# Token stage: the next image's row norm placed between the adds of this image's last products, GELU results in two buffers, tokens taken two images ahead

## The reference

```python
t = x.reshape(B, H * W, dim)                       # after the group norm
t = gelu(t @ W1 + b1); t = gelu(t)                 # 48 -> 16, GELU twice
x1, x2 = t[..., :8], t[..., 8:]
n = layernorm(x2, gamma, beta)                     # over 8 numbers: the "row norm"
sp = depthwise_conv3x3(n) + dw_b                   # the "band"
ch = conv1x1(n) + pw_b
out = (x1 * (sp * ch)) @ W2 + b2                   # 8 -> 48, added to x
```

## Time and profile before

| | us |
|---|---|
| median of 3 runs (2686.31 to 2691.76) | 2691.73 |
| the profiled execution, its own time | 2685.25 |
| its span in the trace | 2683.4 |
| TensorE busy | 2388.4 (89%) |
| VectorE busy | 1330.0 (50%) |
| ScalarE busy | 798.8 (30%) |
| GpSimd busy | 211.3 (8%) |

### The profile page before, as it was taken

How to read it: one execution, slowest core, us unless ns; L and a number is a source line. 1 busy time by engine, 2 the same in 40 slices (tenths; PEclk the granted TensorE clock), 3 DMA queues, 4 the chain that set the end, 5 groups by cost and what they waited for, 6 DMA issues and landing times.

```text
span 2683.4 us, 45712 instructions
## 1 busy us (share of the span) xinstructions
PE 2388.4 (89%) x18588; PEld 2129.1 (79%) x18588; DVE 1330.0 (50%) x3212; ACT 798.8 (30%) x1240; POOL 211.3 (8%) x260
## 2 busy tenths in 40 slices
PE   1999999999999999999999991799999999943785
PEld 1999957956963499999999991799999999942453
DVE  3323344345346544444555558544444555567855
ACT  3533354344245530244002443300441000002441
POOL 2000000000000181000000006300000000000321
PEclk9999999999999999999999996899999999976898
DMA  8840000004000440000000007500000000049734
GB/s 151 154 86 8 1 1 1 1 1 90 6 1 0 94 72 1 1 1 1 1 1 1 1 1 239 126 1 1 1 1 1 1 1 1 1 129 278 240 110 125
DMA packets 80040, 129.89 MB, mean 48 GB/s; under 512 B 10577, under 2 KB 59953, under 8 KB 76945
## 3 DMA queue, kind: packets, MB, share of 16 engines
q1 hardware_dynamic: 72544, 123.36, 19.2%
q10 hardware_dynamic: 7184, 3.84, 0.6%
q0 software_dynamic: 128, 0.01, 0.0%
HBM read 76.85 MB, written 50.33 MB: 47 GB/s over the span
## 4 chain that ended last, share of the span: by engine, by line
PE 82%; DVE 9%; ACT 3%; DMA 2%; SPq 1%; issue 1%; POOL 0%; ACTq 0%; DVEq 0%; POOLq 0%
PE bank L1003 18%; PE bank L1004 16%; PE bank L1005 16%; PE bank L904 14%; PE bank L966 6%; PE bank L919 3%; PE bank L909 3%; DVE stats L1133 3%; ACT work L665 3%; PE bank L1111 2%; DMA work<-in_x 1%; SPq L355 1%; PE bank L1082 1%; DVE band L1252 1%; DVE image L1342 1%
## 5 line engine op out<-in xcount | busy, mean ns | idle before, releaser
L1328 DVE TENSOR_TENSOR image<-bank,image 112x128 f32<-112x128 f32 x2032 | 660.5, 325 | 712.6 <-PE bank L1005 712.6
L1003 PE MATMUL bank<-image,scan_wt 112*112 112x128 f32 x4064 | 810.5, 280 | 9.8 <-ACT image L762 6.7
L1004 PE MATMUL bank<-image,scan_wt 112*112 112x126 f32 x4064 | 771.7, 271 | 0.0
L1005 PE MATMUL bank<-image,scan_wt 112*112 112x126 f32 x4064 | 770.7, 270 | 0.0
L1004 PEld LDWEIGHTS bank<-image,scan_wt 112*112 112x112 f32 x4064 | 581.9, 176 | 0.0
L1005 PEld LDWEIGHTS bank<-image,scan_wt 112*112 112x112 f32 x4064 | 579.4, 176 | 0.0
L1003 PEld LDWEIGHTS bank<-image,scan_wt 112*112 112x112 f32 x4064 | 567.2, 175 | 15.3 <-ACT image L762 7.1
L665 ACT ACTIVATE work<-image,gn_shift,gn_scale 48x567 f32<-48x567 f32 (+5 forms) x384 | 334.9, 905 | 329.4 <-PE bank L909 220.4
L904 PE MATMUL bank<-work 112*128 112x192 f32 x2304 | 422.9, 332 | 10.5 <-issue 10.5
L904 PEld LDWEIGHTS bank<-work 112*128 112x128 f32 x2304 | 374.0, 192 | 12.9 <-issue 12.5
L758 ACT COPY work<-image 48x256 f32 x192 | 80.4, 419 | 686.0 <-PE bank L1005 685.6
(11 more groups left out here) (154 smaller groups left out, 1498.8 us busy)
## 6 DMA issues: line engine op xcount, KB each, us to landing
work<-saved SPq DMA_DIRECT2D x64, 384.0 KB, 9.3
image<-flat_rows SPq DMA_DIRECT2D x4, 3072.0 KB, 18.5
out<-image SPq DMA_DIRECT2D x8, 1536.0 KB, 7.3
flat_rows<-image SPq DMA_DIRECT2D x46, 192.0 KB, 6.5
saved<-image SPq DMA_DIRECT2D x20, 384.0 KB, 8.1
band<-in_x SPq DMA_DIRECT2D x16, 384.0 KB, 5.6
work<-in_x SPq DMA_DIRECT2D x16, 384.0 KB, 5.8
saved<-image SPq DMA_DIRECT2D x8, 768.0 KB, 8.1
```

Source lines behind the costliest of these rows:

```text
L1003: mm(dst, wt[:, 1], src, start=True, stop=False)
L1004: mm(dst[:, 1:J2, :], wt[:, 0], src[:, 0:J2 - 1, :], start=False, stop=False)
L1005: mm(dst[:, 0:J2 - 1, :], wt[:, 2], src[:, 1:J2, :], start=False, stop=True).then_inc(s_prod[g], 1)
L1328: v.tensor_tensor(line(g, along_w, at), prod, line(g, along_w, src), ALU.add).then_inc(s_state[g], 1)
```

## The change

The hidden values get two buffers: `hid[0]` in the free columns behind image 0's tokens, as before, and `hid[1]` in those behind image 2's. All sixteen token groups of image 1 run before the loop over images, with its GELU behind them. The groups of image 2 stand in image 0's second half of products, two behind each product. Those of image 3 stand eight ahead of image 1's gate turn and eight in image 1's first half of products, two behind each of the last four. Each image's hidden values are turned one image earlier. The four parts of the next image's row norm stand behind certain adds, by the table `AHEAD` (key: half f and product q; value: part); for image 3 the first two parts stand ahead of image 2's gate. ScalarE's queue is rearranged to match.

```diff
-EARLY = 12
+AHEAD = ({(0, 0): (0,), (0, 2): (1,), (0, 6): (2,), (1, 1): (3,)},
+         {(0, 0): (0,), (0, 2): (1,), (0, 6): (2,), (1, 1): (3,)},
+         {(0, 0): (2,), (0, 3): (3,)},
+         {})
...
-        hid = image[:, TCOLS:IMG]
+        hid = [image[:, i * 2 * IMG + TCOLS:(i * 2 + 1) * IMG] for i in range(2)]
...
-            def mlp(b, more, even_more):
-
+            def take_hidden(b):
+                if b == 1:
+                    act.wait_ge(s_flat[1][0], 32 * (NBLK - 1))
+                    act.wait_ge(s_taken, 4)
                 for i in range(2):
                     act.wait_ge(s_hid_t, b * 4 + (i + 1))
-                    nc.scalar.copy(*hidden_views(i)).then_inc(s_hid_a, 1)
-                for g in range(6 if more else 0):
-                    take_tokens(b + 1, g)
+                    nc.scalar.copy(*hidden_views(b, i)).then_inc(s_hid_a, 1)
+
+            def row_deviation(b):
                 act.wait_ge(s_ln, b * 2 + 1)
                 nc.scalar.activation(s4, s3, ACT.Sqrt).then_inc(s_ln_a, 1)
-                for g in range(6, EARLY if more else 0):
-                    take_tokens(b + 1, g)
+
+            def mlp(b):
 
                 act.wait_ge(s_ln, b * 2 + 2)
                 nc.scalar.copy(n_pad[:, :, 1:1 + W].rearrange("p c (q w) -> p q c w", q=NQ),
                                spm.rearrange("p (q c w) -> p q c w", q=NQ, c=G)).then_inc(s_ln_a, 1)
                 take_turned(b, 1, n_t)
-                for g in range(EARLY, GROUPS if more else 0):
-                    take_tokens(b + 1, g)
+                if b == 1:
+                    gelu_twice(2)
+                    affine(3)
+                    take_hidden(2)
+                    for g in range(8):
+                        take_tokens(3, g)
+                if b == 2:
+                    take_hidden(3)
+                    row_deviation(3)
                 take_turned(b, 7, g_t)
                 if b == 0:
                     deviation(7, 2, NB, 128)
-                if more:
-                    gelu_twice(b + 1)
-                if even_more:
-                    affine(b + 2)
+                    take_hidden(1)
+                    affine(2)
+                    row_deviation(1)
+                    for g in range(GROUPS):
+                        take_tokens(2, g)
+                if b == 1:
+                    for g in range(8, GROUPS):
+                        take_tokens(3, g)
+                    row_deviation(2)
+                    gelu_twice(3)
...
+            take_hidden(0)
+            for g in range(6):
+                take_tokens(1, g)
+            row_deviation(0)
+            for g in range(6, GROUPS):
+                take_tokens(1, g)
+            gelu_twice(1)
             for b in range(NB):
-                mlp(b, b + 1 < NB, b + 2 < NB)
+                mlp(b)
...
+            def tokens(b, g0, g1, flush=True):
 
                 for g in range(g0, g1):
-                    turn_tokens(g)
-                    if g % 4 == 0 and g > g0:
-                        hidden(g // 4 - 1)
-                hidden(g1 // 4 - 1)
-
-            def mlp(b, more):
-
-
+                    turn_tokens(b, g)
+                    if g % 4 == 0 and g and g != 8 * (b == 3):
+                        hidden(b, g // 4 - 1)
+                if flush:
+                    hidden(b, g1 // 4 - 1)
...
+            def turn_hidden(b):
                 pe.wait_ge(s_gelu, b * 5 + 5)
                 for i in range(4):
                     for t in range(4):
                         o = i * 512 + t * 128
                         last = nc.tensor.transpose(bank[2 + i][:, t * 128:(t + 1) * 128], hid_t[:, o:o + 128], ident)
                     last.then_inc(s_hid_t, 1)
-                if more:
-                    pe.wait_ge(s_xn, b + 2)
-                    tokens(b + 1, 0, EARLY)
+
+            def mlp(b):
...
                     if q % 4 == 3:
                         last.then_inc(s_gt_p, 1)
+                if b == 2:
+                    turn_hidden(3)
                 pe.wait_ge(s_add, b * 2 * NQ + TWO)
                 pe.wait_ge(s_ln_a, b * 2 + 2)
...
-                if more:
+                if b < 2:
+                    turn_hidden(b + 1)
+                if b == 1:
                     pe.wait_ge(s_pw_used, b * 2 + 2)
-                    tokens(b + 1, EARLY, GROUPS)
+                    pe.wait_ge(s_xn, 4)
+                    tokens(3, 0, 8)
 
                 pe.wait_ge(s_gate, b + 1)
...
+                        if b == 0 and f == 1:
+                            if q == 0:
+                                pe.wait_ge(s_xn, 3)
+                            tokens(2, 2 * q, 2 * q + 2, q == NQ - 1)
+                        if b == 1 and f == 0 and q >= 4:
+                            o = 8 + 2 * (q - 4)
+                            tokens(3, o, o + 2, q == NQ - 1)
 
             pe.wait_ge(s_xn, 1)
-            tokens(0, 0, GROUPS, False)
+            tokens(0, 0, GROUPS)
             pe.wait_ge(s_band, N_BAND + G + 1)
-            mlp(0, True)
-            for b in range(1, NB):
-                mlp(b, b + 1 < NB)
+            turn_hidden(0)
+            pe.wait_ge(s_xn, 2)
+            tokens(1, 0, GROUPS)
+            for b in range(NB):
+                mlp(b)
...
-            def mlp(b, more, behind=None):
-
-                for i in range(4):
-                    row_norm(b, i)
-                    if behind and i < 2:
-                        behind(NBLK + 3 + i)
-                for t in range(5, NBLK if behind else 0):
-                    last = behind(NBLK + t)
-                    if t == NBLK - 1:
-                        last.then_inc(s_taken, 2)
+            def mlp(b):
+
+                if b == 2:
+                    row_norm(3, 0)
+                    row_norm(3, 1)
...
                                         ALU.add).then_inc(s_add, 1)
+                        for i in AHEAD[b].get((f, q), ()):
+                            row_norm(b + 1, i)
...
-            mlp(0, True, rows_stats)
-            for b in range(1, NB):
-                mlp(b, b + 1 < NB)
+            for i in range(4):
+                row_norm(0, i)
+                if i < 2:
+                    rows_stats(NBLK + 3 + i)
+            for t in range(5, NBLK):
+                last = rows_stats(NBLK + t)
+            last.then_inc(s_taken, 2)
+            for b in range(NB):
+                mlp(b)
```

## The result

| | kernel before | changed kernel |
|---|---|---|
| median of 19 runs, us | 2689.18 (2683.94 to 2695.04) | 2700.73 (2694.99 to 2709.59) |
| ratio, 95% interval | 1 | 1.0044 [1.0035, 1.0053] |
| profiled execution: span, its own time, us | 2683.4, 2685.25 | 2702.6, 2704.45 |
| token stage: first norm copy to the end, us | 204.51 | 215.60 |

The account below looks back on a forecast made before the run. In the token stage neither TensorE nor VectorE is full: row norm, turn, band, gate and products with adds run one behind the other. Six terms sum to +6.7 us on 2688.8, giving 2696; range 2687 to 2706.

Parts of the forecast that it names:

- start: First norm copy to image 0's first product: GELU ahead of the padding copy delays band and gate; +6.0, bounds +5.0 and +7.1.
- image 0: First product to the next turn: TensorE bounds the second half; 36.5 us against 34.40, +2.1, bounds 33.2 and 39.0 us.
- image 1's turn: Turn to first product: eight groups of image 3 delay the gate's turn; +6.8, bounds +6.3 and +7.5, called the surest.
- image 2: Its turn to image 3's turn: 38.6 us against 45.59, -7.0, bounds 36.4 and 41.5; includes 1.3 more beside GpSimd.
- much slower: Rival: TensorE falls towards half clock in every product stage; +15 in the middle, +19.6 at most, 2704 us; chance 0.18.
- image 1's products: First product to the next turn: square root queued behind the last token copy; 33.0 us against 32.37, +0.6.
- Image 3: Its turn to the end: turn and band no longer follow a 15 us stop; -1.8, bounds -1.8 and 0.
- Without a term: Second hidden buffer and earlier residual loads on SP's queue: no lasting wait added, loads stay hidden, so no time counted.
- The table load: Table switches on ScalarE: 1.28 us each without drain; the skill's drain rule would add 4.1, making the sum near +11.
- Faster: Rival: VectorE sets the pace in both product stages, token groups riding in TensorE's waits; -13.8, 2675 us; chance 0.10.
- No change: Rival: TensorE stays at 2.4 GHz and GpSimd misses the norm; -0.1, 2689 us; chance 0.18.
- the change doesn't do what it says: Rival: second hidden region comes free late, GELU results wait and all slides back; 2689 us; chance 0.04.

Follow-up runs that it names:

- kernel 1: Changed kernel with image 1's two GELUs moved on ScalarE's queue behind image 0's padding copy and n copies: 2696.26 us, 1.0019 to the kernel before.
- kernel 5: Changed kernel with the edits of kernel 1, kernel 2, kernel 3 and kernel 4 together: 2679.80 us, 0.9962 to the kernel before.
- kernel 8: kernel 5 with GpSimd's b2 additions for images 1 to 3 also held until that image's row norm is done: 2679.60 us, 0.9954 to the kernel before.
- kernel 7: Changed kernel with 32 unread transposes filling TensorE's wait for image 0's padding copy, ahead of the band: 2699.04 us, 1.0031 to the kernel before.
- kernel 4: Changed kernel with image 2's token groups behind image 0's products five to twelve, and image 1's square root after two copies: 2694.97 us, 1.0018 to before.
- kernel 2: Changed kernel with no image 3 token groups ahead of image 1's gate turn, all sixteen behind its products five to twelve: 2697.87 us, 1.0031 to before.
- kernel 3: Changed kernel with image 2's square root moved ahead of the last six token copies on ScalarE: 2697.57 us, 1.0032 to the kernel before.
- kernel 6: Changed kernel with GpSimd's b2 additions for images 1 to 3 held until that image's row norm is done: 2695.70 us, 1.0014 to before.

## Why the prediction was right and wrong

The sign and the places were right: the time lies in the range, and three of the six terms came out within 1 us. The size was 11.1 in place of 6.7. The missing 4.4 is start +2.8, image 0 -2.2, image 1 +0.6 (0.8 and -0.2) and image 2 +3.1, each rounded. Three stretches came out above the bounds that I gave them: the start (+8.8 against at most +7.1), image 1's turn (+7.6 against +7.5, the term that I called the surest) and image 2 (41.73 against 41.5). In time the result lies nearer to the middle of the rival "much slower" (2704) than to the forecast (2696); what speaks against that rival is two stretches, image 0 and image 1's products, for which it had +4.6 and +4.5 at the most, and which came out at -0.1 and +0.4.

*Start: mechanism right, +6.0 against +8.8.* The step that failed is "the last token copy ends near 2496.6", 17.7 behind the first norm copy. The trace has 2506.9, or 19.9. What the step left out is TensorE's clock in the groups: where they ran at full speed, in kernel 1, the copy ended at 17.73. In the changed kernel the last eight groups come right behind a wait of 3.40 for a token copy that stood behind the square root (2496.05), and begin at a granted clock of 0.52, near the 1.2 GHz level: four transposes take 1.09 where they take 0.64 elsewhere. Then GELU takes 5.2 as worked out, and the padding copy starts 25.13 behind the norm copy instead of 16.72. The band waits 4.22, as forecast, and takes 7.19 at 0.57; I had put up to 1.8 for that, and taken less. So 8.4 comes through the queue and the slow groups, 1.7 from the band (7.19 less 5.52), and the gate gives back some 1.1 without GpSimd beside it, as forecast (its last step takes 1.88 in place of 3.04). Kernels 1, 5 and 8 show the order as the cause, and kernel 7 prices the clock in the band at 2.3 to 2.9.

*Image 0: +2.1 against -0.1, the low part of its bounds.* Its second half is bound by TensorE as forecast: from 2547.4 to 2567.4 it is busy 17.27 of 20.00 us, and in kernel 4, where part of this work moves forward, the stretch is 3.3 shorter. The tenth product goes 17.15 behind the first (2550.26), between the 16.1 and 19.9 of the working, and the rest takes 17.15 on 18.2 of counted work. The 2.2 that I had put on top of this for GpSimd and the clock is what was too much. GpSimd's addition (2540.46 to 2554.8) fell on parts 2 and 3 instead of part 1, where they lie mostly beside the groups, and these ran at 2.4 GHz (1.00 over the same 20 us) in place of the slow beginning that I had allowed for.

*Image 1, turn to first product: mechanism right, +6.8 against +7.6.* The affine ends 12.5 behind the turn (2579.91), as worked out from rows of before; the gate's turn starts at 21.8 instead of the 20.9 of the sum, since the first groups behind the wait of 2.65 ran slowly (granted 0.93 over the stretch). In kernel 1, at 1.00, the stretch takes 21.90. Kernel 2 takes the groups away and gives 7.2 back.

*Image 1, products: right, +0.6 against +0.4.* The root behind the last copy cost 5.25 of waiting, and kernel 3 gives back 4.3. The lower bound was 30.6 with this wait and no slow clock; the other 2.1 fits with TensorE's 0.50 in 2597 to 2602, where four multiplies take 2.93 instead of 1.57 (12.60 / 8), and with the last step of part 0, which takes 2.17 instead of 1.23 beside GpSimd's addition (2584.29 to 2595.75). No run separates these two.

*Image 2: the mis-sized term, -7.0 against -3.9.* The step was "beside GpSimd 1.3 more". L1466, L1468 and L1469 take 2.47, 2.46 and 3.02 beside the addition, and 1.23, 1.22 and 1.87 without it: 3.6. I had scaled from one operation of the earlier trace rows, where three were in the way. The trace of before had the price: L1429 takes 2.49 there, and its like L1431 1.23 in the earlier trace rows; each of the three should have carried the difference. The Trainium skill, "SBUF — State Buffer", "SBUF: two separate sides", states the rule that I didn't weigh: VectorE operations with two SBUF inputs and GpSimd share a pair of ports under a lock that one instruction holds to its end, and the other blocks. This case agrees: the two-column operation ahead of the stage ends with GpSimd's addition both times (1658.85 and 1658.83, 1660.40 and 1660.38), and here each of the three pays 1.15 to 1.24, less than one of GpSimd's eight instructions alone (11.46 / 8 = 1.43), while RECIPROCAL (one input; 0.95) and the adds (one input in PSUM, the banks that TensorE writes; 0.56) pay nothing. The remaining part of the term was right in kind: products behind waits of 3 and 4 us start slowly, and when the waits shrink the stretch falls to 35.60 (kernel 6), under my lower bound of 36.4.

*Image 3: right, -1.8 against -1.77.* The turn takes 1.04 in place of 1.97 and the band 5.56 in place of 6.46, as worked out.

*Without a term: right.* Image 1's norm copies (2535.36) start as its first add ends, so the hidden results weren't late, and image 3's addition on GpSimd ends at 2657.5, ahead of its first add at 2682.6.

*The table load.* The Trainium skill, "ScalarE: Activation LUTs", "What ACT_TABLE_LOAD costs", would have made the sum +11, which is what was measured. That is chance: GELU again began 1.30 behind the start of a load of 1.28 (2506.92, 2508.22), and the square root 1.29 behind its own (2608.51, 2609.80), with no drain between, and both loads begin within 0.02 of the end of the copy ahead of them; the queue, the clock and GpSimd account for the time.

*The rivals.* Faster (VectorE sets the pace) needed under 12 us for the second half of image 0; it took 20.0. It fell. No change fell: it needed the low ends of the start and image 2, and both came out above the high ones. That the change doesn't do what it says fell too: the hidden results were in time. Much slower (half clock in every product stage) was partly true: 0.74 and 0.75 were granted in image 1's products and image 2, where before had 0.87, and 0.50 in 2597 to 2602, but image 0's 0.84 is no worse than before's 0.82, so the stage that it needed most didn't slow.

## What to carry to other kernels

Before moving long work forward on an in-order engine, list what stands behind it there and who waits for that: a GELU of 5.2 us ahead of a 1.1 us copy cost 7.4 to 8.2, with the slow clock behind the wait that it made, and eight groups ahead of one turn 7.2. Together that is more than the 11.4 by which the stage beats before's once the queues are mended (kernel 5). Put a short link of another engine's chain (a square root, a padding copy) ahead of the bulk work. And when work is put beside another engine, price each instruction of it by its like that already stands there in the trace, not the group by one.

## What was not expected of the hardware

- GpSimd's addition also pays: 11.46 when VectorE has no steps with two SBUF inputs in that time (kernel 6), 14.94 beside the three of image 2.
- TensorE held the full clock through a wait that was filled with unread transposes (granted 1.00 from 2505 to 2520 in kernel 7): the band took 5.62 behind 3.66 us of them, and 7.19 to 8.53 behind the idle 4.22.
- One stretch ahead of the stage took 74.3 to 82.9 us over ten profiled executions of kernels with the same code there, and all of the spread lies in nine VectorE operations that can meet an addition of GpSimd; a subtraction of two columns took 0.16 alone and up to 4.45 there (kernel 8). That is more than most of the effects here; a comparison of two whole spans would have put 8 us of it down to the change.
